# Joining the two halves of the embedding-table sum on VectorE, its average in the last pair's fifth unit, and the first experts' preparation inside the last projection

## What is computed

```python
h = concat([tok(x), txt], axis=1)                     # 8 sequences of 178 rows, 192 wide
# attention on xn = layernorm(layernorm(h), ln_w)
avg_wte = mean(wte, axis=0)
Q    = xn[:, None] * W_qk[None, :, None, :]           # 12 heads
attn = softmax(causal(Q @ Q.T / sqrt(192)))
out  = (attn @ (xn - avg_wte)) * 1 / arange(1, 179)
h    = h + out.reshape(...) @ W_o.T
# experts on x = layernorm(h)
scores = softmax(x @ gate_w + gate_b)                 # 16 experts in 8 groups
w_full = 2.5 * scores of the best 4 experts within the best 4 groups, else 0
y = sum_e silu(x@Wu_e+bu_e) * (x@Wg_e+bg_e) * w_full_e @ Wd_e + w_full @ bd
h = h + y + silu(x@sWu+sbu) * (x@sWg+sbg) @ sWd + sbd # one shared expert, 17 in all
```

## Time and profile before

| | |
|---|---|
| median of three timed runs | 476.73 us (476.62 to 477.12) |
| the profiled execution's own time | 476.07 us |
| its span (first to last instruction) | 474.2 us |
| PE busy | 448.3 us (95%) |
| DVE busy | 279.2 us (59%) |
| ACT busy | 181.8 us (38%) |
| POOL busy | 97.5 us (21%) |
| mean granted TensorE clock | 0.977 of full speed |
| moved by DMA | 65.01 MB, mean 137 GB/s |

### The profile page before, as it was taken

How to read it: one execution, slowest core, us unless ns; L and a number is a source line. 1 busy time by engine, 2 the same in 40 slices (tenths; PEclk the granted TensorE clock), 3 DMA queues, 4 the chain that set the end, 5 groups by cost and what they waited for, 6 DMA issues and landing times. The chain is left out here.

```text
span 474.2 us, 7663 instructions
## 1 busy us (share of the span) xinstructions
PE 448.3 (95%) x2836; PEld 403.3 (85%) x2836; DVE 279.2 (59%) x789; ACT 181.8 (38%) x581; POOL 97.5 (21%) x110
## 2 busy tenths in 40 slices
PE   8699999999999999982998999989999999999997
PEld 7488779877898778972866999989999999999996
DVE  4488866476654976304497635697447654754443
ACT  1467566256644376411445035532312232121211
POOL 3012122221122211210013015921180027000000
PEclk9799999999999999996799999999999999999999
DMA  8968999999999999978316022322323222222220
GB/s 208 252 242 155 212 214 213 213 214 214 213 213 215 212 214 214 212 138 200 133 38 238 1 74 67 64 47 65 86 63 64 63 85 59 60 73 72 75 65 25
DMA packets 23686, 65.01 MB, mean 137 GB/s; under 512 B 2876, under 2 KB 13332, under 8 KB 23266
## 3 DMA queue, kind: packets, MB, share of 16 engines
q0 software_dynamic: 7904, 40.86, 41.1%
q1 hardware_dynamic: 14882, 22.68, 17.9%
q10 hardware_dynamic: 864, 1.00, 0.7%
HBM read 61.88 MB, written 1.27 MB: 133 GB/s over the span
## 5 line engine op out<-in xcount | busy, mean ns | idle before, releaser
L805 PE MATMUL bank<-woT,area_o 128*128 128x192 f32 (+1 forms) x432 | 71.9, 327 | 0.0
L520 ACT ACTIVATE pm<-bank,nmax 128x128 f32<-128x128 f32 x96 | 34.5, 369 | 96.2 <-DVE nmax L1024 96.2
L1110 DVE TENSOR_TENSOR area_b<-area_b,area_w 128x356 f32<-128x356 f32 x64 | 33.9, 529 | 62.7 <-ACT area_b L585 62.6
L805 PEld LDWEIGHTS bank<-woT,area_o 128*128 128x128 f32 (+1 forms) x432 | 69.8, 182 | 0.6 <-issue 0.6
L422 POOL DMA_DIRECT2D area_w<-in_L_attn_wte_dram x26 | 31.4, 1226 | 127.7 <-DMA area_w<-in_L_attn_wte_dram 127.7
L887 PE MATMUL bank<-area_w_r,area_o_r 128*128 128x356 f32 x112 | 43.9, 392 | 0.0
L585 ACT ACTIVATE area_b<-bank,area_k 128x356 f32<-128x356 f32 x32 | 17.8, 558 | 58.9 <-PE bank L891 58.9
L754 PE MATMUL bank<-pT,xn 128*128 128x356 f32 x96 | 39.7, 495 | 0.0
L543 ACT ACTIVATE area_b<-xb,w 64x192 f32<-64x192 f32 x96 | 38.3, 447 | 0.8
L923 PE MATMUL bank<-area_k,area_b 128*128 128x192 f32 (+1 forms) x192 | 36.8, 327 | 0.0
L888 PE MATMUL bank<-area_w_r,area_o_r 128*128 128x356 f32 x112 | 36.4, 325 | 0.0
(11 more groups left out here) (218 smaller groups left out, 1019.4 us busy)
## 6 DMA issues: line engine op xcount, KB each, us to landing
area_w<-in_L_attn_wte_dram POOLq DMA_DIRECT2D x28, 1344.0 KB, 12.6
area_w<-gate_rows SPq DMA_DIRECT2D x64, 178.0 KB, 3.0
area_k<-in_experts_dram SPq DMA_DIRECT2D x8, 353.0 KB, 6.5
area_a<-in_experts_dram SPq DMA_DIRECT2D x6, 353.0 KB, 5.1
woT<-in_L_attn_W_o_dram SPq DMA_DIRECT2D x1, 1728.0 KB, 15.9
area_o<-in_x_dram SPq DMA_DIRECT2D x4, 384.0 KB, 9.1
area_w<-area_w POOLq DMA_DIRECT2D x1, 1344.0 KB, 9.8
area_b<-in_experts_dram SPq DMA_DIRECT2D x3, 353.0 KB, 6.4
```

Source lines behind the costliest of these rows:

```text
L520: act.activation(pm[:, sl, n, :], SIDE[k][:, j * P:(j + 1) * P], ACT.Exp, bias=nmax[:, sl, n:n + 1], accum_out=psums[:, sl, n:n + 1])
L805: last = pe.matmul(o, oT[:, c, at:at + n], woT[:, c, :], start=(c == 0), stop=(c == NCH - 1))
L1110: dve.tensor_tensor(sil[:, n % 2, :], sil[:, n % 2, :], wbc[:, m % RING, :], ALU.mult).then_inc(weighted, 1)
```

## The change

The transfer that added one buffer to the other is gone. VectorE adds them instead, in two halves of seven rows, at the ends of units 1 and 2 of the last pair; its fold to seven and four rows is at the end of unit 3. `mean()` stands in unit 4 before `turn_probs(4)` and `mean_projected()` behind it. SP waits for both sides of the table before the expert loads. `correct(0)` stands after `tails_out(5)`, `experts_in(0)` after `mix_out(5)`, and `correct(1)` after the first two `w_stack`. The last projection is cut: 12 products, `turn_a(0)`, 6 products, `turn_b(0)`, 5 products, `gate(0)`, 13 products, the 18 of the third tile, and then `turn_rows(0)`. ScalarE's `features_a(0)` and `features_b(0)` come after its `mix_out(5)`.

```diff
@@ SP
-            sp.wait_ge(wte_fold, 16)
+            for side in range(2):
+                sp.wait_ge(wte_in[side], 8 * NCHUNK)
@@ POOL
-            for side in range(2):
-                pool.wait_ge(wte_in[side], 8 * NCHUNK)
-            pool.dma_start(wacc[:, 0], wacc[:, 1], accum_op=ALU.add,
-                           max_dma_last_dim=4 * WR * E // 2).then_inc(wte_fold, 16)
@@ ACT
                     if u == 4 and last:
-                        features_a(0)
                         w_high(1)
...
-                if last:
-                    features_b(0)
...
+            features_a(0)
+            features_b(0)
             w_high(2)
@@ PE
-                    if u == 1 and last:
+                    if u == 4 and last:
                         mean()
-                    if u == 2 and last:
-                        mean_projected()
                     turn_probs(u, U + u)
                     if u == 4 and last:
-                        turn_a(0)
+                        mean_projected()
...
                 turn_probs(5, U + 5)
-                if last:
-                    turn_b(0)
...
                 if last:
                     pe.wait_ge(s_small2, 80)
+                    project(i, 0, 0, 12)
+                    turn_a(0)
+                    project(i, 0, 12, NCH)
+                    turn_b(0)
+                    project(i, 1, 0, 5)
                     gate(0)
-                project(i, 0)
-                project(i, 1)
-                if last:
+                    project(i, 1, 5, NCH)
+                    project(i, 2)
                     turn_rows(0)
-                    project(i, 2)
+                else:
+                    project(i, 0)
+                    project(i, 1)
@@ DVE
+                    if u == 4 and last:
+                        dve.wait_ge(avg_psum, 1)
+                        dve.tensor_copy(avg[:], bank[7][:, 0:2]).then_inc(avg_ready, 1)
...
                     if last:
-                        if u == 0:
+                        if u == 1:
+                            for side in range(2):
+                                dve.wait_ge(wte_in[side], 8 * NCHUNK)
+                        if u in (1, 2):
+                            half = slice(WR // 2 * (u - 1), WR // 2 * u)
+                            own.mark(dve.tensor_tensor(wacc[:, 0, half, :], wacc[:, 0, half, :], wacc[:, 1, half, :], ALU.add))
+                        if u == 3:
                             part = wacc[:, 0]
-                            dve.wait_ge(wte_fold, 16)
+                            dve.wait_ge(dve_own, own.at)
                             link(dve.tensor_tensor(part[:, 0:7, :], part[:, 0:7, :], part[:, 7:14, :], ALU.add))
                             dve.tensor_tensor(part[:, 0:3, :], part[:, 0:3, :], part[:, 4:7, :],
                                               ALU.add).then_inc(wsum_ready, 1)
-                        if u == 1:
-                            dve.wait_ge(avg_psum, 1)
-                            dve.tensor_copy(avg[:], bank[7][:, 0:2]).then_inc(avg_ready, 1)
-                        if u == 2:
-                            dve.wait_ge(c_psum, 1)
-                            link(dve.tensor_copy(cbc[:], bank[7][:, E:2 * E]))
-                            correct(0)
-                        if u == 3:
-                            experts_in(0)
-                        if u == 4:
-                            correct(1)
...
                 tails_out(5, U + 5)
                 if not last:
                     maxima(0, U + 6)
+                else:
+                    dve.wait_ge(c_psum, 1)
+                    link(dve.tensor_copy(cbc[:], bank[7][:, E:2 * E]))
+                    correct(0)
                 mix_out(5, U + 5)
...
                 else:
+                    experts_in(0)
                     w_stack(0)
                     w_stack(1)
+                    correct(1)
                     logits(0)
```

More of the change, by code:

```diff
@@ L272, in early_fusion_kernel @@
         wsum_ready = sem("wsum_ready")
-        wte_fold = sem("wte_fold")
         avg_psum = sem("avg_psum")
@@ L788, in turn_rows, with project @@
                 last.then_inc(wT_psum, 1)
-            def project(i, t):
+            def project(i, t, first=0, end=NCH):
                 at, n = COLS[t]
-                if t == 0:
+                if t == 0 and first == 0:
                     pe.wait_ge(ot_act, UPP * i + UPB)
@@ L799, in project @@
                         pe.wait_ge(xnT_ready, 4 * i + 8)
-                if t == 1:
+                if t == 1 and first == 0:
                     pe.wait_ge(ot_act, UPP * (i + 1))
@@ L803, in project @@
                 o = projected(i, t)
-                for c in range(NCH):
+                for c in range(first, end):
                     last = pe.matmul(o, oT[:, c, at:at + n], woT[:, c, :], start=(c == 0), stop=(c == NCH - 1))
-                last.then_inc(wo_done, 1)
+                if end == NCH:
+                    last.then_inc(wo_done, 1)
             turn_in(0, 0, 0)
```

## The result

The changed kernel takes **461.56 us** (median of four runs, 460.6 to 462.42) where the kernel before takes 476.68 beside it: a ratio of 0.9683, 95% interval 0.9661 to 0.9706, 15.1 us. Measured again with other experiments it took 461.04 against 476.94, ratio 0.9674 (0.9645 to 0.9702). The forecast was 462.4, within 460.8 to 466.5. The profiled execution is 461.32 with a span of 459.5 us.

The account below looks back on a forecast made before the run. The prediction took TensorE's queue plus the hole as the bound. Its terms, 9.93 + 1.6 + 2.0 + 1.05 - 0.3 = 14.3 us, off the profiled 476.07 gave 461.8, hence a median of 462.4 us, range 460.8 to 466.5.

Parts of the forecast that it names:

- The forecast case: All terms together: gain of 14.3 us, median of 462.4 us; chance 0.70.
- the hole: TensorE's idle time before `mean()` in unit 1 of the last pair; all 9.93 us counted as gained.
- `mean()` at full clock: `mean()`, moved to unit 4, takes 2.4 us in place of 4.04 at half clock; 1.6 us gained.
- the slow restart: From `turn_probs(1)` to the first mask product after the hole: 2.34 us in place of 4.34; 2.0 us gained.
- waits at the end of the last pair: Four TensorE waits in units 3 to 5, 1.90 us, of which 0.85 remains; 1.05 us gained.
- the cut projection: Last projection: 0 us lost, with slack of 1.2 us at `turn_a(0)` and 2.0 us at `turn_rows(0)`.
- the first expert steps: After the projection, `weigh(1)` waits 0.9 us for its broadcast row; 0.3 us charged as loss.
- VectorE's added work: Two adds of 1.56 us in units 1 and 2 of the last pair hide; 0 us lost.
- The preparation: Rival: its waits surface between projection products, one link being 3 us longer; 465.0 us, chance 0.15.
- VectorE did not bind: Rival: VectorE bounds units 1 to 3, its adds can't hide, 4.7 us come back; 467.1 us, chance 0.07.
- The slower case: Rival: the hole reopens inside the projection, which runs at low clock; 23 us lost, 485.4 us, chance 0.03.
- The clock case: Rival: clock falls in unit 4 at `mean()` and its transposes; 3.6 us of gains come back, 466.0 us, chance 0.05.

## Why the prediction was right, and where it wasn't

The forecast case came true; the terms, start to start, in the two profiled executions:

| term | forecast | measured |
|---|---|---|
| the hole | 9.93 | 10.10 |
| `mean()` at full clock | 1.6 | 1.86 |
| the slow restart | 2.0 | 2.00 |
| waits at the end of the last pair | 1.05 | 1.92 |
| the cut projection | 0 | -0.17 |
| the first expert steps | -0.3 | about 0 |
| sum | 14.3 | 15.7 |

- **The hole.** Measured from where `turn_probs(1)` would have stood (205.74 + 6.28 = 212.02) to `mean()`'s start, 222.12. It is closed in full, and VectorE's wait for the table costs nothing. The experiments add to my reading of the change: it is the place of `mean()` that closes the hole (same stretch with either join), and the join on VectorE is free rather than useful.
- **`mean()` at full clock.** 4.04 to 2.18 us. I took 2.4 for fear of an issue limit in the short passes. The ten 128-column passes halved (2.22 to 1.13 us) and the twenty 64-column ones nearly did (1.82 to 1.05).
- **The slow restart.** 215.60 - 213.26 = 2.34 us, the figure of the earlier trace rows.
- **The last pair's waits were mis-sized**, the largest error. I had added the idle times that the rows name, 1.90, and subtracted 0.85. But the profile counts idle time from a modelled end of the product before, which lies after the next one could have started. Counted from start to start, the four places of the earlier trace rows lost 0.99, 0.73, 0.53 and 0.65 us, 2.90 in all. The first of them is unit 3, 248.99 - 241.72 = 7.27 us long where a unit without waits has 6.28; the row names only 0.46 of its 0.99. After the change one wait is left, printed as 0.77, where the starts show 240.72 - 239.68 = 1.04 less the 0.11 that a transpose takes, 0.93. `mean_projected()` took 0.07 us longer, and with the rounding that leaves 1.92. The experiment that filled the wait bears this out: it brought 1.11 us, more than the 0.77 printed.
- **VectorE's added work**: nothing, as forecast, at one half a unit, and 1.09 us with two in one unit (3.01 us of work). That agrees with the 0.99 us that unit 3 really lost to the 2.9 us of `correct(0)`, where the prediction read 0.46.
- **The cut projection**: from the end of `mix(5)` to the first expert product it took 19.78 us; before, the same work took 19.61 (277.61 - 258.62 and the two transposes, 0.31 each). So 0.17 us were lost, without a wait that the profile names. `turn_a` had 0.82 us of slack where I worked out 1.2. The chain was 0.4 us longer because the first normalization took 0.79 us in place of 0.36, beside POOL's `w_low(0)`, which now comes at the same moment (244.42). `turn_rows` had 2.03 (forecast 2.0). And the uncut version cost about 5 us of waits and over 4 of clock.
- **The first expert steps**: `weigh(1)` waited 1.07 (0.9 forecast), and `down(1)` came 270.08 - 263.14 = 6.94 us after the first product (7.0 before). The 0.3 charged wasn't lost.

The sum came out 1.4 us short in the stretch, and the later start of that execution (1.24 us) hid it from the span; in the medians 15.1 and 15.9 us stand against 14.3.

**The rivals.** The preparation did not surface, though it came nearer than worked out. VectorE did not bind. The slower case needs a wait of over 5 us in the projection. The uncut version had 3.1 us there and two short ones behind it: the clock came back after 10.2 us, not at the experts, and with 470.55 it was still 6 us faster than before. The clock case did not come true in the changed kernel, but a neighbour showed its fall, so 0.05 was a low chance for it. I argued that transposes and 16-column gate passes don't lower the clock, and that the rule on transposes (the Trainium skill, TensorE: Matmul & The Clock Gate, "Part 4: PE-mode transpose") would make it likelier; in the experiment with `mean()` three times over the clock fell within the one-column products, before any transpose, so these were what I should have priced. At three times `mean()`'s length all five runs show the loss; at its own length one profile of nine shows a fall behind it. No run here tests the rule on transposes by itself.

## What to carry over

When an engine waits for a long chain, ask first whether the consumer can stand later in its own queue: here that (with the work behind it moved too) was worth as much as moving it and shortening the chain together, while a faster chain alone (the join on VectorE) got half, because a hole of 2.85 us still cost the clock. Work that then comes late must be cut into what runs beside it, at points worked out from the chain's durations; three cuts in the projection held 9.5 us. And waits are better priced from start to start of the instructions around them than by the idle times that the profile prints.

## What was unexpected in the hardware

- TensorE's granted clock fell to half although the engine was busy without a gap, in ninety passes of one column (`mean()` three times over: busy 9.00 of 9.00 us at 0.50). A fall of the clock need not have a wait in front of it.
- The clock fell after 4.5 us of idling in the kernel before (212.0 to 216.5), after 3.0 us with only the join moved (211.8 to 214.8), and with the uncut projection after 3.3 us (242.2 to 245.5) and 0.4 us of transposes.
- Once fallen, the clock stayed at half for 3.4 us with both halves in unit 1, 6.8 with only the join moved and with the filled hole, 10.2 with the uncut projection and with `mean()` three times over, and 13.7 before the change. TensorE was at work for all or most of that in each but the last.
- The same instructions up to the last pair took 204.54 to 206.98 us in thirteen executions. The granted clock of the stretch from 12 to 24 us was 0.86 in the shortest of them and 0.61 in the longest. In the other eleven it was 0.72 to 0.74, and these still range from 205.10 to 206.29, so this stretch accounts for the two ends at most.

```profile
12.00:24.00 12.00, 8.46 (x42) 6.48 (x42) 6.32 (x15) 5.79 (x19) 1.05 (x2) 0.86 0.85 245
```

```profile
12.00:24.00 12.00, 7.35 (x24) 4.97 (x26) 5.54 (x18) 4.91 (x14) 1.13 (x1) 0.61 0.91 244
```

The first row is that of the first profile with the last wait filled, the second that of the changed kernel's first one.
